# Two of eight B times u products of a selective scan moved from VectorE to GpSimd, and loads of x issued in two parts

## The reference

```python
        def _ssm_scan(dA, dBx, C):
            def step(h, inp):
                dA_t, dBx_t, C_t = inp
                h = dA_t * h + dBx_t
                y = jnp.einsum('bdn,bn->bd', h, C_t)
                return (h, y)
            ...
        def _mamba_block(x, in_w, conv_w, conv_b, A_log, xd_w, xB_w, xC_w, dtp_w, dtp_b, D, out_w, g, b):
            ...
            delta = jax.nn.softplus(xc @ xd_w @ dtp_w + dtp_b)
            Bm = xc @ xB_w
            Cm = xc @ xC_w
            A = -jnp.exp(A_log)
            dA = jnp.exp(delta[..., None] * A)
            dBx = (delta * xc)[..., None] * Bm[:, :, None, :]
            y = _ssm_scan(dA, dBx, Cm) + D * xc
            return y * jax.nn.silu(z) @ out_w + res
```

## Time and profile before

| | before |
|---|---|
| median of 2 runs | 12012.34 us (12010.73 to 12013.96) |
| span of the profiled execution | 12009.0 us |
| busy in that span: VectorE | 10589.0 us (88%) |
| TensorE | 10054.5 us (84%) |
| ScalarE | 6727.0 us (56%) |
| GpSimd | 94.9 us (1%) |
| first instruction of the tail phase on GpSimd | at 10230.57 us |

### The profile page before, as it was taken

One profiled execution on the slowest core, in us unless ns is written; L12 is line 12 of the kernel. 1 busy time (PEld: TensorE's weight loads), 2 busy tenths in 40 slices (PEclk: granted clock), 3 DMA queues, 4 the chain that ended last, 5 costly groups with the idle time before them and its releaser, 6 DMA issues. The chain is left out here.

```text
span 12009.0 us, 120889 instructions
## 1 busy us (share of the span) xinstructions
PE 10054.5 (84%) x41304; PEld 7884.7 (66%) x41304; DVE 10589.0 (88%) x8817; ACT 6727.0 (56%) x10429; POOL 94.9 (1%) x167
## 2 busy tenths in 40 slices
PE   6888888888888888888888888788888887799998
PEld 5666666666666666666666666666666665577776
DVE  6999999999999999999999999999999999233332
ACT  5555555555555555555556555555555654344443
POOL 0000000000000000000000000000000000000000
PEclk8999998999999998989999999999999998899999
DMA  2211122222222112222222211222222221000000
GB/s 78 76 65 60 64 76 71 74 69 69 76 69 72 61 63 70 76 71 76 67 74 71 76 58 62 70 76 71 71 72 69 72 71 36 24 10 10 11 11 9
DMA packets 357683, 728.06 MB, mean 61 GB/s; under 512 B 143670, under 2 KB 188890, under 8 KB 357082
## 3 DMA queue, kind: packets, MB, share of 16 engines
q1 hardware_dynamic: 343128, 683.98, 17.0%
q0 software_dynamic: 10240, 33.56, 0.9%
q10 hardware_dynamic: 3714, 2.89, 0.1%
HBM read 699.27 MB, written 21.05 MB: 60 GB/s over the span
## 5 line engine op out<-in xcount | busy, mean ns | idle before, releaser
L892 PE MATMUL y_ps<-hb,ident 128*128 128x257 f32 x16384 | 4535.9, 425 | 1502.1 <-DVE hb L688 1495.2
L892 PEld LDWEIGHTS y_ps<-hb,ident 128*128 128x128 f32 x16384 | 3311.8, 209 | 2544.2 <-DVE hb L688 2028.9
L679 DVE TENSOR_TENSOR_SCAN hb<-decay,hb 128x1028 f32<-128x1028 f32 x2048 | 4686.6, 2288 | 22.4 <-issue 20.8
L505 ACT ACTIVATE decay<-delta,neg_a 128x512 f32<-128x512 f32 x4096 | 2683.7, 712 | 2196.8 <-DVE hb L679 1620.6
L688 DVE TENSOR_TENSOR hb<-hb,c_all 128x1028 f32<-128x1028 f32 x2048 | 2495.8, 1219 | 0.0
L669 DVE TENSOR_TENSOR hb<-b_all,u_buf 128x1028 f32<-128x1028 f32 x2048 | 2462.5, 1202 | 5.8
L783 PE MATMUL w_ps<-xn,in_w 128*128 128x257 f32 x4096 | 1011.8, 394 | 133.3 <-ACT xn L406 114.9
L783 PEld LDWEIGHTS w_ps<-xn,in_w 128*128 128x128 f32 x4096 | 800.7, 197 | 284.1 <-issue 127.4
L783 PE MATMUL w_ps<-xs_pad,diag_store 128*128 128x257 f32 x4096 | 954.8, 379 | 0.1
L783 PEld LDWEIGHTS w_ps<-xs_pad,diag_store 128*128 128x128 f32 x4096 | 774.1, 189 | 114.1 <-ACT diag_store L426 0.9
L783 PE MATMUL w_ps<-sz,out_w 128*128 128x257 f32 x2048 | 511.1, 393 | 0.8 <-DVE sz L696 0.8
(11 more groups left out here) (238 smaller groups left out, 9669.1 us busy)
## 6 DMA issues: line engine op xcount, KB each, us to landing
b_all<-bc_dram SPq DMA_DIRECT2D x512, 514.0 KB, 3.6
c_all<-bc_dram SPq DMA_DIRECT2D x512, 514.0 KB, 4.9
in_w<-in_L_attn_in_w SPq DMA_DIRECT2D x64, 1024.0 KB, 5.0
x_in<-in_x POOLq DMA_DIRECT2D x128, 256.0 KB, 2.9
out_w<-in_L_attn_out_w SPq DMA_DIRECT2D x64, 512.0 KB, 3.9
h_mid<-h_cur SPq DMA_DIRECT2D x32, 257.0 KB, 3.2
h_F<-h_mid SPq DMA_DIRECT2D x16, 514.0 KB, 3.8
out<-o_sb SPq DMA_DIRECT2D x64, 86.0 KB
```

What stands on the lines that cost most here:

```text
L505: last = func(decay[:, u % NDA, i, :, 1:S], delta[:, c, :, 1:S], ACT.Exp, scale=neg_a[:, k, c, NU * n + i:NU * n + i + 1])
L679: dve.tensor_tensor_scan(h, decay[:, u % NDA, :, :, :].rearrange("p n b s -> p (n b s)"), h, 0.0, ALU.mult, ALU.add).then_inc(scan_done, 1)
L892: last = pe.matmul(y_ps[c % 2][:, b, 0:S], ident[:, :], hb[:, u % NHB, i, b, :], start=False, stop=(n == PAIRS - 1 and i == NU - 1))
```

## The change

- GpSimd forms B times u for the state pairs 3 and 7 of every chunk, which are 8 of the 32 units of a job. It waits for the pair's B (in the first chunk), for `u_buf` and for `y_added` of unit u - 4, and raises `pool_b_done`, a new semaphore.
- VectorE leaves those units' product out; its scan waits for `pool_b_done` there and for `b_done` elsewhere. After the scans of the units with n = 2 and n = 6, C times h of the same unit comes next in its stream.
- The loads of x: tiles 0 and 1 of the next group are issued at the start of the third job, tiles 2 to 7 behind GpSimd's product of unit 11. They stand in the same instruction stream as the products. The first group's loads stay as they were, ahead of everything.

```diff
+POOL_PAIRS = (3, 7)
...
-            def load_x(g, jj):
-
-                for n in range(8):
+            def load_x(g, jj, tiles):
+
+                for n in tiles:
...
+            def b_times_u(g, jj, u):
+
+                c, n = u // PAIRS, u % PAIRS
+                if c == 0:
+
+                    pool.wait_ge(bc_loaded[n], in_registers(pool, job_count(g, jj, 32, 32))[0])
+                pool.wait_ge(u_ready, job_count(g, jj, CI, c + 1))
+                if positive(job_count(g, jj, UNITS, u + 1 - NHB)):
+
+                    pool.wait_ge(y_added, job_count(g, jj, UNITS, u + 1 - NHB))
+                pool.tensor_tensor(hb[:, u % NHB, :, :, :].rearrange("p n b s -> p n (b s)"),
+                                   b_all[:, n, :, :, :].rearrange("p n b s -> p n (b s)"),
+                                   u_buf[:, c % 2, :, :].rearrange("p b s -> p (b s)").unsqueeze(1).to_broadcast([P, NU, T]),
+                                   ALU.mult).then_inc(pool_b_done, 1)
+
             def period(g, jj, first, last):
-                if jj == 2 and not is_final(g):
-                    load_x(g, 4)
-
-            run(pool, lambda: load_x(0, 0), period, lambda g: None)
+                more = jj == 2 and not is_final(g)
+                if more:
+                    load_x(g, 4, (0, 1))
+                for u in range(UNITS):
+                    if u % PAIRS in POOL_PAIRS:
+                        b_times_u(g, jj, u)
+                    if more and u == 11:
+                        load_x(g, 4, range(2, 8))
+
+            run(pool, lambda: load_x(0, 0, range(8)), period, lambda g: None)
...
@@ in b_times_u of VectorE
+                if n in POOL_PAIRS:
+                    return
...
@@ in scan of VectorE
-                dve.wait_ge(b_done, job_count(g, jj, UNITS, u + 1))
+                n = u % PAIRS
+                taken = len([v for v in range(u + 1) if v % PAIRS in POOL_PAIRS])
+                if n in POOL_PAIRS:
+                    dve.wait_ge(pool_b_done, job_count(g, jj, CI * len(POOL_PAIRS), taken))
+                else:
+                    dve.wait_ge(b_done, job_count(g, jj, UNITS - CI * len(POOL_PAIRS), u + 1 - taken))
```

More of the change, by code:

```diff
@@ L208, in mamba_phase @@
         b_done = sem("b_done")
+        pool_b_done = sem("pool_b_done")
         scan_done = sem("scan_done")
```

## The result

| | before | after |
|---|---|---|
| median | 12012.34 us | 12472.53 us (2 runs, 12470.58 to 12474.48) |
| ratio to before | | 1.0379 (1.0358 to 1.0400) |
| span of the profiled execution | 12009.0 us | 12472.9 us |
| VectorE busy | 10589.0 us | 11003.0 us |
| GpSimd busy | 94.9 us | 1910.5 us |

The changed kernel is 460 us slower. VectorE has 512 instructions fewer and is busy 414 us longer.

What follows compares the result with a forecast made beforehand. VectorE, 99.7% busy, was taken to bound the Mamba phase. The span of 12009 us plus 620 for the blocked products and 17 for the loads gave 12646, forecast as 12650 us at the median; range 11950 to 12800 us.

Steps and rivals of the forecast that it cites:

- the deciding term: GpSimd's delay of VectorE for each product in the Mamba phase: 0 to the whole 2.14 us; the whole was taken.
- the blocked case: VectorE stands for GpSimd's whole 2.14 us: +1.21 us a product, +620 us; range 12560 to 12800 us; chance 0.65.
- The bound and what is removed: VectorE alone sets the Mamba phase's time; 512 products leave its stream at 1.12 us each, 573 us.
- The bare dependence: C times h right behind its scan, no longer covered by B times u: 0.11 us each, 56 us added.
- GpSimd's duration: One GpSimd product of 1028 elements takes 2.14 us; all 512 are 1096 us, 11% of the phase.
- In time: GpSimd's product is normally ready for its scan: 7.0 us available, three times its need, so no stall.
- The reason that I gave: GpSimd's memset needs 0.835 ns an element, its product some 1.9, as if two inputs came by one path.
- part sharing: VectorE loses half of 2.14 us: +0.06 us a product, 12060 us at the median, spanning 11800 to 12500; chance 0.18.
- the free rival: GpSimd doesn't delay VectorE in the units: -517 us, plus loads and TensorE's limit, 11575 us; chance 0.17.
- The loads of x: Scan 15 waits about 3.2 us behind them in 15 groups: 48 us undelayed, +17 us at the blocked end.
- the 32 us for TensorE's limit: Half a microsecond a job where TensorE has no gap and VectorE runs up against the four `hb` buffers.

## Why the prediction was right, and what was off

The sign, the bound and the kind of the deciding term came out as forecast. The size didn't: 12472.5 us lies in the stated range, but 177 us under the sum and under the blocked case's own 12560 to 12800.

**The bound and what is removed.** Right. VectorE stayed the limit, and -573 us closes the account.

**The bare dependence.** Right. In the changed kernel C times h behind its scan starts 2.32 us after it (median of 386), where the next instruction started 2.21 us after the scan: 0.11 us.

**GpSimd's duration.** Estimated at 2.14 us; undisturbed it takes 2.18 to 2.19. Small, and right that a broadcast input doesn't matter.

**In time.** Right. But for the first scans after the loads of x no scan waits for GpSimd, though its products take up to 6.59 us with the time that they stand. TensorE's share fell and the four `hb` buffers kept their slack.

**The deciding term.** The end chosen was the right one, and its size was too large: I had +2.14 + 0.08 us of delay for each product, 2.22, and the mean is 1.84 us. Three things make the difference. A refused product of VectorE is mostly 1.97 to 1.99 us longer, 0.2 less than GpSimd's own 2.18, and the overlap with the next instruction isn't lost (5117.39 + 3.20 = 5120.59 us, with the next start at 5120.52); the handover costs nothing on top. The reason that I gave, two inputs that come by one path, wasn't tested: a copy of 1026 elements takes GpSimd 1.03 us undisturbed and the product 2.18, which fits it and doesn't show it. 53 products are let in at an instruction with a PSUM input and cost about 1.3 us, a case that I had set aside as 173 of 9972 us: the instructions are few, but GpSimd, waiting at a boundary, gets in at them far oftener than their share of the time. And 15 meet VectorE while it waits. 512 x 2.22 = 1137 us were counted and 944 measured, 193 less; for the loads 17 were counted and 33 measured. Together that is the distance between 12650 and 12472.5 us. The measured time lies in the stated range, in what was held for part sharing by its size; the mechanism isn't sharing, since every instruction of VectorE with both inputs in SBUF that met GpSimd's reading stood for nearly all that was left of it.

**A row that was there.** The prediction says that the trace of before has no row of the deciding case. It has one, in the tail phase, where GpSimd adds the two halves of `h_F` (L1219) while VectorE adds the two halves of `sq_A`, all in SBUF:

```profile
10323.34 1.09 POOL L1219 TENSOR_TENSOR rstd_F<-h_F 128x514 f32<-128x514 f32 x1 [73.49 <-DMA h_F<-h_mid]
10324.14 0.85 DVE L1408 TENSOR_TENSOR sq_A<-sq_A 128x514 f32<-128x514 f32 x1 [1.22 <-ACT sq_A L1259]
```

The other 47 additions of this line take 0.69 to 0.70 us. VectorE starts with 0.30 us of GpSimd's instruction left and is 0.15 us longer. In the run in which GpSimd only writes, 0.72 us is left at the same place and VectorE takes 1.27 us, 0.57 longer. The overlap is in eleven of the traces, and in each the refused instruction pays what is left of GpSimd's, less 0.15 us, though the engines share no tensor there. This row speaks against the free rival, and for less than the whole 2.14 us.

**The loads of x.** 3.2 us were expected for each of 15 scans, and 33.4 / 15 = 2.2 us measured. The step that failed took TensorE's lag from the trace of before. In the changed kernel VectorE has lost 2 us at unit 11 and TensorE has caught up by 0.9 of them: the issue of tile 7 ends 20.2 us after scan 11 starts in the kernel before and 19.3 us after it in the changed one. With pair 7 alone, where unit 11 has no product on GpSimd, it is 20.2 us again, and the waits are 47.7 / 15 = 3.2 us, the figure of the prediction.

**The free rival.** It gave 11575 us; the run in which GpSimd only writes took 11552. That the two are so close is luck in part. Without the 32 us for TensorE's limit the terms give some 11540 us; VectorE has no wait for TensorE in that run's Mamba phase, and that its instructions are up to 5 ns longer in the mean makes up more than the 12 us left. The premise fell, and no run shows the 32 us.

**What decides whether two instructions meet.** GpSimd's reading costs a refused product of VectorE 1.97 us, its memset 5 ns at most, and L726 keeps its 0.69 us. The Trainium skill, SBUF — State Buffer, section Who interferes with whom, says that an instruction of VectorE with two SBUF inputs contends with one of GpSimd that reads SBUF and not with one that only writes, and that one of VectorE with at most one SBUF input, outside the modes in which it uses two ports, doesn't. The runs agree with each part. L726 and L733 both have their other input in PSUM; no run was made with one SBUF input and nothing in PSUM.

**Open.** Where GpSimd is let in isn't explained. Of the changed kernel's products, waiting ones were let in at a change from a scan to B times u nearly always (204 times, once passed by), from B to C times h mostly (217, 72 passed by), and at a change from C times h to a scan hardly ever (3, about 105 passed by). Copies were let in at that change 118 times and passed by 102 times. No run here was made to tell why. Nor is it shown why the price is some 0.2 us less than what GpSimd's instruction takes.

## What to carry to other kernels

Before work is moved from a saturated VectorE to GpSimd, look at the inputs on both sides: with both of VectorE's in SBUF, GpSimd's reading comes out of VectorE's time, and the move pays only if GpSimd holds VectorE for less time than it relieves it of, here 1.84 us in the mean against 1.01. Judge it by the unchanged instructions' durations in the trace, not by waits, since the refused engine looks busy. In these runs a memset was free beside it, and so was a product of 256 elements made ready early enough to lie under an instruction with a PSUM input. A single overlap of this kind may already stand in the trace of before, as that of L1408 did here.

## What the runs showed of the hardware

- The exclusion grows with what GpSimd reads: 1.97 to 1.99 us for two inputs of 1028 elements, 0.90 to 1.04 for two of 514, and 0.84 us at most for one of 1026, each 0.05 to 0.2 us less than GpSimd's instruction takes alone (2.18, 1.09 and 1.03 us). A memset of 1026 elements costs VectorE nothing.
- Whoever is refused shows it in its own duration, on either engine: a two-element product on GpSimd 1560 ns in the mean, C times h on VectorE 3.20 us.
- Beside a busy VectorE, GpSimd is let in only as VectorE changes instructions, and not at every change; in the changed kernel it waited up to 4.4 us (6.59 less 2.19).
